# A decoder layer in eight batches on one core: the second iteration written out

## What is computed

```
x = x + attn(norm(x))            # 16 heads; softmax over the sequence, each head a causal Toeplitz product
x = x + xattn(norm(x), context)  # keys and values from the batch's context, causal mask, one head
x = x + ffn(norm(x))             # 2 shared experts, and 16 routed ones of which each row uses 2
```

## Time and profile before

| | us |
|---|---|
| median of 3 runs | 573.54 |
| lowest and highest of them | 573.17, 573.91 |
| the profiled execution | 573.51 |
| its span, from the first to the last instruction | 571.7 |

### The profile page before, as it was taken

The page is one execution under the profiler, slowest core; times in us unless marked ns, Lnnn a source line. Parts: engine busy times, 40 slices in busy tenths (PEclk is TensorE's granted clock), DMA queues, the critical chain, the costliest instruction groups (busy, mean ns, idle before and its releaser), DMA issues. The chain is left out here.

```text
span 571.7 us, 12923 instructions
## 1 busy us (share of the span) xinstructions
PE 541.9 (95%) x4716; PEld 368.2 (64%) x4716; DVE 426.5 (75%) x1107; ACT 255.7 (45%) x517; POOL 191.8 (34%) x240
## 2 busy tenths in 40 slices
PE   5787889999999999999999999999999998999997
PEld 4565557566685667766786668666866675666455
DVE  5858687868885787868886888778876776677654
ACT  4565546445354254445344445434543334332332
POOL 4215150223542144223522343234421343133123
PEclk9999999999999999999999999999999999999999
DMA  8995595795439903694449743993189125300351
GB/s 256 308 367 194 182 386 180 155 322 183 112 82 251 335 17 101 148 292 151 111 100 249 242 110 77 204 310 98 51 177 325 57 74 126 64 1 1 86 102 37
DMA packets 90734, 94.70 MB, mean 166 GB/s; under 512 B 28224, under 2 KB 76224, under 8 KB 90432
## 3 DMA queue, kind: packets, MB, share of 16 engines
q1 hardware_dynamic: 90688, 94.09, 58.1%
HBM read 75.66 MB, written 12.12 MB: 154 GB/s over the span
## 5 line engine op out<-in xcount | busy, mean ns | idle before, releaser
L694 POOL TENSOR_TENSOR mid<-gated,mid 128x512 f16<-128x512 f32 x72 | 86.6, 1202 | 214.0 <-ACT mid L880 213.9
L880 ACT ACTIVATE mid<-gated 128x512 f16<-128x512 f32 x72 | 44.9, 624 | 83.3 <-DVEq L1225 80.0
L146 PE MATMUL wide<-w_d,mid 128*128 128x256 f16 x288 | 78.5, 273 | 0.0
L148 PE MATMUL wide<-w_d,mid 128*128 128x256 f16 x288 | 78.5, 273 | 0.0
L147 PE MATMUL wide<-w_d,mid 128*128 128x256 f16 x288 | 78.5, 272 | 0.0
L1203 DVE SCALAR_TENSOR_TENSOR gated<-gated,score 128x512 f32<-128x512 f32 x72 | 49.1, 682 | 37.6 <-ACT gated L875 37.5
L146 PE MATMUL rows<-h3T,w_gu 128*128 128x512 f16 x160 | 60.7, 379 | 0.3 <-DVEq L126 0.3
L146 PE MATMUL score<-h3T,w_gu 128*128 128x512 f16 x160 | 60.7, 379 | 0.2
L147 PE MATMUL rows<-h3T,w_gu 128*128 128x512 f16 x160 | 60.6, 379 | 0.0
L148 PE MATMUL rows<-h3T,w_gu 128*128 128x512 f16 x160 | 60.6, 379 | 0.0
L148 PE MATMUL score<-h3T,w_gu 128*128 128x512 f16 x160 | 60.6, 379 | 0.0
(11 more groups left out here) (249 smaller groups left out, 1402.8 us busy)
## 6 DMA issues: line engine op xcount, KB each, us to landing
toep<-z_scratch SPq DMA_DIRECT2D x14, 2048.0 KB, 18.3
stage<-comb_scratch SPq DMA_DIRECT2D x32, 512.0 KB, 8.5
toep<-z_scratch SPq DMA_DIRECT2D x4, 1024.0 KB, 11.2
x_bo<-in_x SPq DMA_DIRECT2D x8, 512.0 KB, 11.8
x_in<-in_xr SPq DMA_DIRECT2D x7, 512.0 KB, 11.1
qT<-q_scratch SPq DMA_DIRECT2D x7, 512.0 KB, 3.9
vx<-v_scratch SPq DMA_DIRECT2D x7, 512.0 KB, 5.2
out<-x_out SPq DMA_DIRECT2D x7, 512.0 KB, 3.0
```

What stands on the lines that cost most here:

```text
L146: pe.matmul(out, stationary[0], moving[0], start=start, stop=False, **kw)
L148: return pe.matmul(out, stationary[1], moving[0], start=False, stop=stop, **kw)
L694: pool.tensor_tensor(mid_slot(j, 1, late), gate_slot(j, late), mid_slot(j, 0, late), ALU.subtract).then_inc(mid_split.sem, 1)
L880: act.activation(mid_slot(j, 0, late), gate_slot(j, late), ACT.Copy).then_inc(mid_hi.sem, 1)
```

## The change

Iteration 1 is written out for each engine as `second_iteration`, and the branches and tables for it go. Against the order before:

- PE makes both value products (v0, v2) ahead of the Toeplitz product, and both remaining units of context 1 behind the transposes of the mixed heads; three units of context 2 stand ahead of the transposes of h2, its last and the first of context 3 behind them; of contexts 3 and 4 single units stand between the steps of scores, probabilities and attention, and half of context 5 stands behind the transposes of h1.
- POOL makes the reciprocal deviation of h2 ahead of context 3's low part, and takes the low parts of two pieces of gate weights (128x1024 each) over from DVE, each in two instructions (a product with the scale in place, and a subtraction).
- Scores 0 to 3 of batch 0 use the banks of `score` in turn (`score_use`), where s1, s2 and s3 had the same bank.
- Batch 2's rows are normalised by ACT (`normalise_x`) with a shift from POOL (`make_shift_x`), not by DVE.
- SP waits for all four DMAs of batch 0's Toeplitz rows, and then issues x, context 2, the gates' second half, context 3 and the down weights.

```diff
 AHEAD = 3
-
-CONTEXT_AT = {5: (4, (0, 1)), 6: (4, (2, 3)), 7: (5, (0, 1)), 8: (5, (2,))}
-
-CONTEXT_BEFORE = {3: (3, (2,)), 4: (3, (3,))}
...
+        LATE = len(pieces) - LATE_PIECES
+        GATES_2 = LATE - 2
...
+        def score_use(it, c):
+            return ("s0", "s1", "g3", "s2")[c] if one_group(it) else f"s{c}"
...
                     sp.wait_ge(first_toep_loaded, 32)
+                    sp.wait_ge(toep_loaded.sem, toep_loaded.at(it, 32))
+                    load_residual(it)
+                    load_context(2)
                     load_gates(1)
-                    load_context(2)
-                if f and not d:
+                if f and m and not d:
                     load_residual(it)
                 if f and not m:
...
+            def part_weights(some):
+                for i in some:
+                    n, k, at = pieces[i]
+                    name, _, dst, _, _ = loads[n]
+                    pool.wait_ge(w_hi, i + 1)
+                    pool.wait_ge(w_lo, i)
+                    src = staged[name][:, k, at]
+                    pool.tensor_scalar(src, src, X_W, None, ALU.mult).then_inc(w_scaled, 1)
+                    pool.wait_ge(w_scaled, i - GATES_2 + 1)
+                    pool.tensor_tensor(dst[:, 1, k, at], src, dst[:, 0, k, at], ALU.subtract).then_inc(w_lo, 1)
+            def second_iteration(it):
+                add_bias(it - 1)
+                part_context_columns(2)
+                reciprocal_deviation(it - 1, 1)
+                make_shift(it - 1)
+                part_context_columns(3)
+                part_weights(range(GATES_2, LATE))
+                part_context_columns(4)
+                reciprocal_deviation(it + 1, 0)
+                make_shift_x(it + 1)
+                reciprocal_deviation(it - 1, 2)
+                reciprocal_deviation(it - 1, 2, 1)
+                part_context_columns(5)
...
+            def second_iteration(it):
+                part_context(1, (0, 1))
+                part_weights(range(MIDDLE, GATES_2))
+                for g in range(K2):
+                    take_first_mix(g)
+                part_values(it, it, 0)
+                part_values(it, it, 2)
+                part_turned(it, it - 1, mixT, mixT_hi, "mix")
+                part_context_columns(2)
+                part_context(1, (2, 3))
+                z_powers(it)
+                act.wait_ge(w_lo, GATES_2)
+                part_context(2, (0,))
+                part_context_columns(3)
+                part_context(2, (1,))
+                normalise_last(it - 1, it)
+                part_context(2, (2,))
+                part_turned(it, it - 1, h2T, h2T_hi, "h2")
+                part_weights(range(GATES_2, GATES_2 + 1))
+                part_context(2, (3,))
+                part_context(3, (0,))
+                exp_scores(it, it - 1, 0)
+                exp_scores(it, it - 1, 1)
+                part_z(it)
+                part_weights(range(GATES_2 + 1, LATE))
+                part_context(3, (1,))
+                act.wait_ge(ctx_stored[1], 32)
+                part_prob(it, it - 1, 0)
+                exp_scores(it, it - 1, 2)
+                part_context_columns(4)
+                act.wait_ge(w_lo, GATES_2 + 1)
+                part_context(3, (2,))
+                part_prob(it, it - 1, 1)
+                exp_scores(it, it - 1, 3)
+                part_context(3, (3,))
+                part_prob(it, it - 1, 2)
+                part_context(4, (0,))
+                part_prob(it, it - 1, 3)
+                part_context_columns(5)
+                part_context(4, (1,))
+                act.wait_ge(w_lo, LATE)
+                part_context(4, (2, 3))
+                normalise_x(it + 1)
+                part_turned(it, it - 1, h3T, h3T_hi, "h3")
+                part_context(5, (0, 1))
+                part_turned(it, it + 1, h1T, h1T_hi, "h1")
+                part_context(5, (2, 3))
...
+            def second_iteration(it):
+                b = it - 1
+                rows.take(dve, it, "v0")
+                part_context(1, (0, 1))
+                part_weights(range(MIDDLE, GATES_2))
+                z_max(it)
+                part_values(it, it, 0)
+                part_values(it, it, 2)
+                rows.take(dve, it, "o0")
+                part_turned(it, b, mixT, mixT_hi, "mix")
+                turned.take(dve, it, "h2.0")
+                part_context(1, (2, 3))
+                add_residual(it, 0)
+                aggregate(b, 1, add_residual(it, 2))
+                part_context(2, (0,))
+                normalise(b, it, 1, x_res, h2)
+                z_invert(it)
+                score.take(dve, it, "s0")
+                part_context(2, (1, 2))
+                part_turned(it, b, h2T, h2T_hi, "h2")
+                part_context(2, (3,))
+                for c in range(2):
+                    score_max(it, b, c)
+                part_context(3, (0,))
+                for c in range(2):
+                    score_sum(it, b, c)
+                part_z(it)
+                part_context(3, (1,))
+                part_prob(it, b, 0)
+                score_max(it, b, 2)
+                x_statistics(it + 1, range(2))
+                score_sum(it, b, 2)
+                part_context(3, (2,))
+                score_max(it, b, 3)
+                part_prob(it, b, 1)
+                attended(it, 0)
+                score_sum(it, b, 3)
+                attended_statistics(it, 0)
+                part_context(3, (3,))
+                part_prob(it, b, 2)
+                attended(it, 1)
+                x_statistics(it + 1, range(2, C))
+                part_context(4, (0,))
+                part_prob(it, b, 3)
+                aggregate(b, 2, attended_statistics(it, 1))
+                attended(it, 2)
+                part_context(4, (1,))
+                attended(it, 3)
+                attended_statistics(it, 2)
+                aggregate(b, 2, attended_statistics(it, 3), 1)
+                normalise(b, it, 2, x_res, h3)
+                part_context(4, (2,))
+                normalise(b, it, 2, x_res, h3, 1)
+                part_context(4, (3,))
+                for banks in (score, rows):
+                    banks.reach(dve, banks.taken, it)
+                part_turned(it, b, h3T, h3T_hi, "h3")
+                part_context(5, (0, 1))
+                part_turned(it, it + 1, h1T, h1T_hi, "h1")
+                part_context(5, (2, 3))
+                turned.reach(dve, turned.taken, it)
...
                     if n and m:
                         if d and j in (3, 4):
                             x_statistics(it + 1, range(2 * (j - 3), 2 * (j - 3) + 2))
-                        if not d and j == 5:
-                            normalise(it + 1, it, 0, x_in, x_in)
...
+            def second_iteration(it):
+                b = it - 1
+                pe.wait_ge(turned.taken.sem, turned.is_taken(b, "h1.1"))
+                z_product(it)
+                project(it, "v0", h1T, w_v)
+                project(it, "v2", h1T, w_v)
+                pe.wait_ge(ctx_taken.sem, ctx_taken.at(1, 2))
+                for g in range(K2):
+                    toeplitz(it, b, g)
+                pe.wait_ge(mix_taken, K2)
+                turn(it, "mix", h2)
+                context(1, (2, 3))
+                project_mix(it)
+                context(2, (0, 1, 2))
+                turn_halves(it, "h2", h2, h_ready[1], b, h2_normed)
+                context(2, (3,))
+                context(3, (0,))
+                pe.wait_ge(ctx_taken.sem, ctx_taken.at(0, UNITS))
+                pe.wait_ge(turned.taken.sem, turned.is_taken(it, "h2.1"))
+                scores(it, 0)
+                scores(it, 1)
+                context(3, (1,))
+                turn_probs(it, b, 0)
+                scores(it, 2)
+                context(3, (2,))
+                turn_probs(it, b, 1)
+                attend(it, 0)
+                scores(it, 3)
+                context(3, (3,))
+                turn_probs(it, b, 2)
+                attend(it, 1)
+                context(4, (0,))
+                turn_probs(it, b, 3)
+                attend(it, 2)
+                context(4, (1,))
+                attend(it, 3)
+                context(4, (2, 3))
+                turn_halves(it, "h3", h3, h_ready[2], b)
+                context(5, (0, 1))
+                pe.wait_ge(h_ready[0].sem, h_ready[0].at(it + 1, 2))
+                turn(it, "h1", x_in)
+                context(5, (2, 3))
+                for banks in (turned, rows, score):
+                    banks.reach(pe, banks.ready, it)
```

189 lines of the change are left out of this document (52 added, 137 removed).

## The result

The changed kernel takes 569.86 us (median of 5 runs, 569.05 to 571.01), the kernel before 573.80 (5 runs, 573.17 to 574.33): a ratio of 0.9931, 95% interval 0.9918 to 0.9943, 3.9 us less. The forecast was 569.2, in a range of 567.6 to 571.5. The profiled execution took 569.86 with a span of 568.1, so 3.6 less span than before.

A forecast was written before the change was run, and what follows sets the result against it. PE bounds the kernel, with 10.8 us of waits in one stretch as all that can be won. Four parts win 4.9, less 0.6 for mixT is 4.3: 573.51 - 4.3 = 569.2 us, range 567.6 to 571.5.

The forecast's parts named there:

- the 0.6 for mixT: Behind the stretch: iteration 2's mixT queues behind up to 1.5 us of other data; 0.6 us taken as loss.
- stays, 50.93: Batch 1's head projection to iteration 2's first Toeplitz product: PE's own work unchanged at 50.93 us, only waits counted.
- (a): Up to the W_O product: waits fall from 3.6 to 1.3 us, 2.3 won; W_O starts near 43.0.
- The issue gap: PE's 1.0 us wait for nothing visible amid Toeplitz products; between 0 and 1.0 would remain, 0.5 taken.
- it also wins little: SP's wait for the Toeplitz rows: costs nothing and wins little, since its rows were first in the queue before.
- (b): From W_O to the scores: waits fall from 2.7 to 0.85 us, 1.85 won.
- reciprocals first: POOL, h2's reciprocals ahead of context 3's low part: wins nothing over the old time, keeps 2 us from being lost.
- (c): Scores to attention: waits fall from 1.95 to 1.7 us, 0.25 won, with 1.45 of new wait before the third turn.
- (d): Attention 3 to iteration 2: waits fall from 2.5 to 2.0 us, 0.45 won.
- The citation ahead of the sum: DVE instructions with two SBUF inputs and POOL instructions reading SBUF exclude each other; half a microsecond goes with DVE's gate-weight piece.
- POOL is dear: Rival: POOL's pieces take 5 to 6.5 us, PE 0.8 to 3.8 later, 570.0 to 573.0, likeliest 570.8; chance 0.10.
- pieces over 4.6: Sign of being wrong: a gate-weight piece on POOL takes over 4.6 us, where 3.4 plus a 0.2 hop was taken.

The follow-up runs named there:

- recip_late: Changed kernel with one edit undone: POOL makes context 3's low part ahead of h2's reciprocal deviation; 572.22 us, ratio 0.9980 to the kernel before.
- best: Changed kernel with context 2 stored early, context 5's low part early, batch 1's softmax part, context 4's parts and context 3's third unit reordered; 564.94 us, ratio 0.9852.
- half_wait: Changed kernel with SP's wait alone undone: loads in the new order, issued once the first two Toeplitz DMAs have landed; 573.99 us, ratio 1.0012 to the kernel before.

## Why the prediction was right, and where it was wrong

**The sum.** Of the 3.6 that the span lost: waits 10.81 to 6.58, 4.23 won (4.9 forecast); 1.15 more, since PE's busy time without what the clock added is 51.42 - 1.64 = 49.78 and not 50.93; 1.64 lost to the clock; 0.36 lost ahead of the stretch, which varies between executions (the head projection starts at 29.4 to 30.5 in the fourteen profiles); 0.22 won behind it. 4.23 + 1.15 - 1.64 - 0.36 + 0.22 = 3.6. That this is only 0.7 from the forecast 4.3 is luck in part: 0.7 less was won in waits, the 0.6 for mixT was not paid, and a gain and a loss of over a microsecond each, neither in the sum, nearly offset each other. The term for the clock was put at nothing because the trace of before had no fall.

**PE's work "stays, 50.93".** It did not. Units issued back to back start 1.31 apart and last 1.47; each wait shows the 0.15 that otherwise lies under the next product. Before had 18 such breaks in the stretch, the change 9: at 0.15 each 1.35, near the 1.15. A wait removed gives back its length and up to 0.15.

**(a) Start to W_O.** Forecast 1.3 of waits and W_O at 43.0 from a start at 29.45, measured 0.7 and 43.24 from 29.81: right but for the gap, taken at 0.5 and absent. The step did not agree with itself: 46.16 less the 2.3 that it counts as won is 43.9, not 43.0. Of waits 2.9 went, not 2.3. "The issue gap has nothing in the order that removes it" was wrong, and so was the sentence on SP's wait, "it also wins little". The mechanism is the fetch, and the term is 2.25 for the new order without the wait, with what the clock adds on top. I had named the held-back loads as "the one thing near it that changes", and then took half the gap without asking what PE does in it.

**(b) W_O to the scores.** Forecast 0.85, measured 0.49 + 0.38 + 0.16 = 1.03; "reciprocals first" as told (recip_late, 2.4).

**(c) Scores to attention.** Forecast 1.7, measured 0.16 + 0.53 + 1.49 = 2.2. The wait before the third turn is as forecast (1.45), at its place. The 0.53, before attention 0, was missing. DVE's softmax part, 1.26 longer beside POOL, stands in the row ahead of it; best, where that part took 0.73, has no such wait, but it moved other work too.

**(d) Attention 3 to iteration 2.** Forecast 0.7 for the first half of h3, 0.9 for the second and 0.45 for a unit. Measured none, 2.27 and none, since the 2.27 and the slow clock hid the last. In number that is near the 2.0 of the sum, by luck; in mechanism this is the step that failed: DVE's instruction took 2.40 because of POOL. The citation ahead of the sum named the exclusion, and it was used for one instruction that went, not for those that POOL's longer row would meet.

**POOL's pieces.** A piece took 2.79 + 2.13 and gaps, 5.2 with the hop, not 3.6. That is the rival "POOL is dear", and by the prediction's own sign, pieces over 4.6, it was wrong here. The rival's price was 0.8 at least; measured 0.34, since ACT had context 4 ready and PE, late by 1.5 before the third turn, asked later. The product, 2.8 to 3.0, was mis-sized by a factor of 2.5: with one input it takes longer than the subtraction with two. The estimate by the Trainium skill (GPSIMD Engine Reference, section "Key points"), 4.9 for a piece and 0.6 for PE, was nearer than mine.

**x and mixT.** x landed 3.5 after its issue (3.7 taken), at 38.97, and the bias took 2.78, not 4.06; PE did not wait. mixT was issued ahead of vx's landing, at 94.62 against 96.20, as forecast, and PE waited 0.25 for it, as before: the 0.6 was not paid.

## What to carry to other kernels

Where an engine waits for nothing in a stretch of many short instructions, look for its instruction fetch among the DMA packets and for the loads in line with it; holding those back decided here whether the new order won anything (569.86 with, 573.99 without), and lost 1.4 in the old order. Before work is moved to POOL, or POOL's work to another time, list what DVE does from on-chip memory alone in that window: each such instruction can cost what is left of POOL's. Take no profile as free of a fall of the clock: read the mean clock of each run, and compare medians only with that beside them.

## What the runs showed of the hardware

- A late fetch costs PE dearly in short products: 158 products went by in 4.3 us, and PE stood 2.25 to 2.51 with 3.5 MB of loads beside the rows, 1.01 in before. PE went on 2.45 to 2.54 after the fetch had begun, in four kernels. The Trainium skill (Runtime: NRT & Kernel Launch, section "Instruction fetch mechanics") calls the crossing of a block mostly hidden; the trace of the change agrees (no gap), half_wait's, with the loads in line, does not (2.25).
- What sets how much a load delays the fetch stays open: counted from the head projection it came at 5.1 in the change (5.1 to 5.7 in the eight kernels with its loads and values), 5.9 with x alone, 8.1 and 8.4 with all; in before's order on PE at 4.5 with the wait and 6.2 without.
- DVE's normalisation with two columns of scalars stands while a POOL instruction runs (2.40 for 0.71, and 0.74 with POOL elsewhere), not only instructions with two tensors from on-chip memory.
- POOL stands too: its product took 3.03 and 3.11 where DVE's softmax part ran at its start, 2.78 and 2.79 elsewhere.
